# Two score groups on two partition halves: paired 64-row products in an attention kernel

## The chip, the cores and the metric

One core of a Trainium2 chip runs the whole program. The metric is the device time of one execution in microseconds, median of three runs.

## The reference, cut to what matters

A batch of 32 items with 128 tokens of 128 channels goes through a modulated linear layer, grouped-query attention (16 heads of width 64 in 4 groups that share keys and values), a second modulated layer with a small attention among the 16 heads of each token, a third modulated layer, and a top-2 mixture of 8 experts. The change is in the attention:

```python
Q = (X @ Wq).reshape(n, s, 4, 4, 64)      # group, head in group, key width
K = (X @ Wk).reshape(n, s, 4, 64)
V = (X @ Wv).reshape(n, s, 4, 64)
raw = einsum('bsgwe,btge->bstgw', Q, K / 8)
attn = softmax(raw, axis=2)               # over the keys t
A = einsum('bstgw,btge->bsgwe', attn, V).reshape(n, s, 1024)
return X + A @ Wpost
```

## The kernel before

The program is written engine by engine; each engine has its own queue in program order, and semaphores tie them. The batch is a software pipeline: slot s (function `slot` of each engine) does the attention core of item s (`B` in the code), projections of item s+1 (`A`), output projection and key mixing of item s-1 (`C`), head mixing of items s-2 and s-3 (`H`, `D`). Slots run from -2 to 34; those from 4 to 29 are a loop that does two slots a turn. Then come routing and an expert loop, in which this change touches nothing.

The scores are computed twice. First in bf16 with queries as rows (`scores`, L580): four products of 128x128 into the one bank `bank_s`, then VectorE takes the maximum over the keys (`group_max`, L292) into four columns of `row_max`. After four groups `row_max` is transposed by TensorE (L666), ScalarE negates it (`neg_max`), and GpSimd spreads it with a mask (L1053) into `neg_diag`: partition 64+h holds head h's negated maxima in its own quarter, zeros elsewhere. Then in fp32 with keys as rows (`scores_t`, L589): a bf16 product of `g_rows` with `neg_diag` starts the bank and puts minus the maximum everywhere, a fp32 product of keys and queries adds the scores. ScalarE takes the exponential out of the bank (`exp_scores`, into `prob`), and `attend` (L597) multiplies with the values; a column of ones gives the denominator, which VectorE inverts (L301) and applies (L306).

The contraction of keys and queries is 64 long, the array has 128 rows. Before, keys and queries of all groups lie on partitions 0 to 63, and partitions 64 to 127 of `qT`, `q16`, `k_one` and `k16` are zeros, so every product is one of 128 rows. Two groups leave the projection on partitions 0 to 63 and 64 to 127 of a bank; ScalarE's copies (`copy_q` L829 and the keys' copy) therefore come in two halves that bring the upper one down. The bf16 twins are made by ScalarE for the queries (`narrow_q`, L858) and by VectorE for the keys (L440). fp32 products appear in the trace as two records, each with its own weight load; bf16 products and transposes as one.

Three PSUM banks (`misc`) serve all the small results in turn; `bank_free` (L217) makes TensorE wait for the readers of a bank's last use. TensorE's order within a slot is written by hand (L644 to L742).

Of the kernel before, what the change touches and what calls it, by code (L numbers as in the profile page):

```python
# [19 lines left out]
HEADS = GROUPS * HPG  # L20
CHUNKS = HEADS * KEY // P
# [15 lines left out]
def build(nc, xT, condT, aff_wT, aff_b, mod_wT, mod_b, wq, wk, wv, wpost, gate_wT,  # L37
          w1, b1T, w2, b2, out):
    ctx = ExitStack()
    with ctx:  # L40
# [16 lines left out]
        own_head = sb("own_head", [P, HEADS])  # L57
        own_w = sb("own_w", [P, HPG])
# [30 lines left out]

        qT = sb("qT", [P, 2, HEADS, P])  # L90
        q16 = sb("q16", [P, 2, HEADS, P], BF16)
        k_one = sb("k_one", [P, 2, GROUPS, P])
        k16 = sb("k16", [P, 2, GROUPS, P], BF16)
# [81 lines left out]
        s_own, s_owned = sem("own"), sem("owned")  # L175
# [31 lines left out]
        def bank_users(bank, s):  # L207


            a, c, h, d = s + 1, s - 1, s - 2, s - 3  # L210
            return ((("q0", a, [(s_q, 4 * a + 2)]), ("q1", a, [(s_q, 4 * a + 4)]),
                     ("kv", a, [(s_v, n(a)), (s_k, 2 * n(a))]), ("y", a + 1, [(s_y_raw, n(a + 1))])),
                    (("att0", c, [(s_attT, 2 * c + 1)]), ("neg", s, [(s_neg, n(s))]), ("kx", c, [(s_kxT, n(c))]),
                     ("kxn", c, [(s_kx2, n(c))]), ("o", d, [(s_tok, n(d))])),
                    (("att1", c, [(s_attT, 2 * c + 2)]), ("post", c, [(s_x1T, n(c))]), ("mix", d, [(s_mixT, n(d))])))[bank]

        def bank_free(eng, bank, s, use):  # L217

            now = bank_users(bank, s)
            at = [u[0] for u in now].index(use)  # L220
            for _, b, readers in (*reversed(now[:at]), *reversed(bank_users(bank, s - 1))):
                if has(b):
                    for sm, v in readers:
                        eng.wait_ge(sm, v)
                    return

# [20 lines left out]
        def qkv_bank(b, use):  # L247

            return misc[("q0", "q1", "kv").index(use)] if s_is(b, 0) else misc[0]
# [5 lines left out]
        def _(dve):  # L255
# [3 lines left out]
            V.memset(k_one[KEY:P, :, :, :], 0.0).then_inc(s_zero, 1)  # L259
            V.memset(k16[KEY:P, :, :, :], 0.0).then_inc(s_zero, 1)  # L260
            V.memset(v1[:, :, :, :], 1.0).then_inc(s_zero, 1)
            V.memset(row_max[:, :], 0.0).then_inc(s_zero, 1)
            dve.wait_ge(s_const, 2)
            V.tensor_reduce(own_w[:, :], own_head[:, :].rearrange("p (g w) -> p w g", w=HPG), AX.X,
                            ALU.add).then_inc(s_owned, 1)
            V.tensor_reduce(own_g[:, :], own_head[:, :].rearrange("p (g w) -> p g w", w=HPG), AX.X,
# [22 lines left out]
            dve.wait_ge(s_zero, 6)  # L289
            dve.wait_ge(s_owned, 3)  # L290

            def group_max(s, g):  # L292
                dve.wait_ge(s_s_mm, 4 * s + g + 1)
                need(dve, s_neg_mm, n(s - 1))
                V.tensor_reduce(row_max[:, KEY + HPG * g:KEY + HPG * (g + 1)], bank_s[:, :, :], AX.X,  # L295
                                ALU.max).then_inc(s_max, 1)
# [56 lines left out]
            def slot(s, j):  # L353
# [3 lines left out]
                if B:  # L357
                    group_max(s, 3)
                if A:
                    dve.wait_ge(s_yT, n(a))  # L360
                    V.tensor_tensor(x_all[:, col(a)], x_all[:, col(a)], yT[:, :], ALU.add).then_inc(s_xy, 1)
                if D:
# [74 lines left out]
                if A:  # L437
                    dve.wait_ge(s_k, 2 * n(a))
                    need(dve, s_s_mm, 4 * n(a - 2))
# [3 lines left out]
                if B:  # L443
                    normalise(s, 0)
                if B:
                    invert(s, 1)
                if A:
                    group_max(a, 0)
                if B:
                    normalise(s, 1)  # L450
                if A:
                    group_max(a, 1)
                if B:
                    invert(s, 2)
                if B:
                    normalise(s, 2)
                if A:
                    group_max(a, 2)
                if B:
                    invert(s, 3)  # L460
                if B:
                    normalise(s, 3)
                if has(a + 1):
                    dve.wait_ge(s_y_raw, n(a + 1))
                    need(dve, s_kv_mm, n(a))
                    need(dve, s_xy, n(a))
                    V.tensor_scalar(yT[:, :], y_raw[:, :], CLAMP, -CLAMP, ALU.min, ALU.max).then_inc(s_yT, 1)  # L467

# [91 lines left out]
        def _(pe):  # L560
# [16 lines left out]
            pe.wait_ge(s_blank, 5)  # L577
# [28 lines left out]
            def queries(b, half):  # L606
                bank = qkv_bank(b, ("q0", "q1")[half])
# [17 lines left out]
            def gate_logits(tiles):  # L625

                bank = bank_s if tiles[0] in EARLY else misc[0]
                pe.wait_ge(s_tok, tiles[-1] + 1)
                for b in tiles:
# [14 lines left out]
            def slot(s, j):  # L644
# [5 lines left out]
                if C:  # L650
                    bank_free(pe, 1, s, "att0")
                    att_transpose(c, 0)
                if B:
                    scores(s, j, 3)
                if C:
                    bank_free(pe, 2, s, "att1")
# [3 lines left out]
                if A:  # L660
                    pe.wait_ge(s_yT, n(a))
                    queries(a, 0)
                if B:
                    bank_free(pe, 1, s, "neg")
                    pe.wait_ge(s_max, 4 * s + 4)
                    nc.tensor.transpose(misc[1][:, 0, :], row_max[:, :], ident[:, :]).then_inc(s_neg_mm, 1)  # L666
                if s_is(s, BATCH - 1):
                    gate_logits(parts_early[0])
                if C:
# [6 lines left out]
                    last.then_inc(s_post_mm, 1)  # L676
                if s_is(s, BATCH):
# [3 lines left out]
                if A:  # L681
                    if not s_is(a, 0):
                        bank_free(pe, 0, s, "q1")
                    queries(a, 1)
                if C:
                    bank_free(pe, 1, s, "kx")
# [4 lines left out]
                if B:  # L691
                    scores_t(s, j, 1)
                if C:
                    pe.wait_ge(s_kxT, n(c))
                    nc.tensor.transpose(misc[1][:, 0, :], kxT[:, :], ident[:, :]).then_inc(s_kxn_mm, 1)
                if D:
                    bank_free(pe, 2, s, "mix")
# [4 lines left out]
                if B:  # L702
                    attend(s, j, 0)
                if s_is(s, BATCH - 1):
# [407 lines left out]
```

## Time and profile before

| | |
|---|---|
| three runs | 666.54, 666.96, 669.44 us; median 666.96 |
| profiled execution | 666.56 us, of which the span 664.8 |
| TensorE, weight loads, VectorE, ScalarE, GpSimd busy | 92%, 73%, 78%, 62%, 43% of the span |
| TensorE's granted clock over the span | 0.972 of 2.4 GHz |
| bytes moved | 7.15 MB, nearly all in the first 25 us and the last 15 us |

The page's 40 slices show TensorE at nine tenths or more from the third slice to the 33rd (33 to 548 us), then a gap (the last items' mixing and the routing), and the expert loop after it. The loop of slots is thus where the time is. A record of TensorE has a modelled end that lies past the next record's start, so durations of records don't add up; distances between starts do. On VectorE and ScalarE too a record of a back-to-back row may reach some 0.1 us into the next one.

### The profile page before, as it was taken

Reading aid. Unit: us, or ns where it says so; the run is one execution under the profiler, and the core shown is the slowest. Engines: PE = TensorE matmul, PEld = TensorE weight load, DVE = VectorE, ACT = ScalarE, POOL = GpSimd, SP = SyncE. Lnnn points to the kernel's source line nnn. Section 1 sums busy time; section 2 is a strip of 40 time slices with the busy share of each in tenths; the row PEclk is TensorE's granted clock in tenths of the full one; section 3 lists DMA queues with packets and bytes.
Section 4 is the critical chain, followed back from the end, with each engine's and each line's share of the span. In section 5 each row is a group of like instructions: output and inputs, shape, how many; then the busy total and the mean of one; then the engine's idle time right before and its main releaser. Section 6 shows DMA issues by size and latency. Waiting matters only on the chain. (4 is left out here: it accounts for less than half of the span.)

```text
span 664.8 us, 14883 instructions
## 1 busy us (share of the span) xinstructions
PE 612.5 (92%) x4212; PEld 488.4 (73%) x4212; DVE 521.2 (78%) x1155; ACT 413.3 (62%) x823; POOL 287.8 (43%) x251
## 2 busy tenths in 40 slices
PE   3799999999999999999999999999999991699998
PEld 3587787777778777878787878787878780557665
DVE  6235888888888888888888888888888879867776
ACT  1666777777777767776666777777777541334443
POOL 5102555555555555555555555555555447000000
PEclk9799999999999999999999999999999995699999
DMA  7100000000000000000000000000000000000004
GB/s 246 45 1 1 1 2 1 1 0 0 0 0 0 0 0 0 0 0 0 0 0 0 0 0 0 0 0 0 0 0 0 2 1 0 1 0 0 0 0 126
DMA packets 9361, 7.15 MB, mean 11 GB/s; under 512 B 1088, under 2 KB 8832, under 8 KB 9216
## 3 DMA queue, kind: packets, MB, share of 16 engines
q1 hardware_dynamic: 9344, 6.94, 3.5%
q8 instruction: 9, 0.15, 0.1%
q14 instruction: 8, 0.07, 0.0%
HBM read 4.84 MB, written 2.10 MB: 10 GB/s over the span
## 5 line engine op out<-in xcount | busy, mean ns | idle before, releaser
L1061 POOL TENSOR_TENSOR pair<-kx 128x1152 f32<-128x1152 f32 x32 | 82.3, 2573 | 164.0 <-ACT kx L805 159.7
L602 PEld LDWEIGHTS bank_a<-v,prob 128*128 128x128 f32 x1024 | 127.1, 192 | 16.7 <-issue 16.2
L602 PE MATMUL bank_a<-v,prob 128*128 128x65 f32 x1024 | 131.7, 272 | 0.0
L594 PE MATMUL bank_t<-qT,k_one 128*128 128x512 f32 x256 | 131.6, 596 | 0.0
L295 DVE TENSOR_REDUCE row_max<-bank_s 128x4 f32<-128x512 f32 x128 | 87.3, 682 | 13.4 <-PE bank_s L585 9.0
L440 DVE CAST k<-k_one 64x512 bf16<-64x512 f32 x32 | 50.0, 1564 | 58.0 <-ACT k_one L805 58.0
L805 ACT ACTIVATE prob<-bank_t 128x512 f32<-128x512 f32 x128 | 76.3, 596 | 29.7 <-PE bank_t L594 26.5
L1041 POOL TENSOR_TENSOR mix_hi<-mix_hi 128x512 f32<-128x512 f32 (+2 forms) x96 | 80.0, 833 | 7.5
L609 PEld LDWEIGHTS misc<-yT,wq_sb 128*128 128x128 f32 x512 | 67.9, 200 | 18.3 <-issue 15.4
L1053 POOL TENSOR_TENSOR neg_diag<-neg_max,own_w 16x512 bf16<-16x512 f32 x32 | 36.3, 1134 | 100.8 <-ACT neg_max L805 86.4
L805 ACT ACTIVATE qT<-misc 64x512 f32<-64x512 f32 x128 | 75.4, 589 | 5.9 <-PE misc L609 3.5
L609 PE MATMUL misc<-yT,wq_sb 128*128 128x128 f32 x512 | 71.1, 285 | 2.4 <-DVE yT L467 2.4
L805 ACT ACTIVATE q<-qT 64x1024 bf16<-64x1024 f32 x64 | 67.2, 1050 | 1.0
L1034 POOL TENSOR_TENSOR mix_hi<-weight,kx 128x1024 f32<-128x1024 f32 x32 | 63.9, 1998 | 4.7 <-ACT weight L805 4.7
L585 PEld LDWEIGHTS bank_s<-k,q 128*128 128x128 bf16 x512 | 33.9, 98 | 40.8 <-DVE row_max L295 20.6
L585 PE MATMUL bank_s<-k,q 128*128 128x128 bf16 x512 | 50.5, 221 | 14.2 <-DVE k L440 12.3
L674 PE MATMUL misc<-attT,wpost_sb 128*128 128x128 f32 x512 | 62.6, 275 | 0.0
L306 DVE TENSOR_TENSOR att<-bank_a,recip_den 128x256 f32<-128x256 f32 x128 | 54.1, 423 | 9.9
L674 PEld LDWEIGHTS misc<-attT,wpost_sb 128*128 128x128 f32 x512 | 60.3, 193 | 0.0
L805 ACT ACTIVATE y_raw<-misc,modb_sb,demod 128x128 f32<-128x128 f32 x32 | 14.6, 457 | 68.8 <-PE misc L739 66.8
L805 ACT ACTIVATE hT<-bank_t,b_now 128x512 f32<-128x512 f32 x42 | 28.9, 687 | 44.7 <-PE bank_t L771 44.6
L594 PEld LDWEIGHTS bank_t<-qT,k_one 128*128 128x128 f32 x256 | 49.1, 192 | 4.6
(153 smaller groups left out, 1069.9 us busy)
## 6 DMA issues: line engine op xcount, KB each, us to landing
out<-acc_all SPq DMA_DIRECT2D x8, 256.0 KB, 2.3
x_all<-in_xT SPq DMA_DIRECT2D x1, 1024.0 KB, 9.8
w_sb<-in_w SPq DMA_DIRECT2D x2, 512.0 KB
x_all<-in_xT SPq DMA_DIRECT2D x1, 768.0 KB, 7.6
wq_sb<-in_wq SPq DMA_DIRECT2D x1, 512.0 KB, 6.2
wpost_sb<-in_wpost SPq DMA_DIRECT2D x1, 512.0 KB, 9.5
x_all<-in_xT SPq DMA_DIRECT2D x1, 256.0 KB, 3.3
b_rows<-in_b SPq DMA_DIRECT2D x16, 4.0 KB
```

The source lines that it names most:

```text
L295: V.tensor_reduce(row_max[:, KEY + HPG * g:KEY + HPG * (g + 1)], bank_s[:, :, :], AX.X, ALU.max).then_inc(s_max, 1)
L306: V.tensor_tensor(att[:, HPG * g:HPG * (g + 1), :], att_bank(g)[:, :, 0:KEY], recip_den[:, g % 2, :].unsqueeze(2).to_broadcast([P, HPG, KEY]),
L440: V.tensor_copy(k16[0:KEY, ja, :, :], k_one[0:KEY, ja, :, :]).then_inc(s_k16, 1)
L585: last = mm(bank_s[:, w, :], q16[:, j, HPG * g + w, :], k16[:, j, g, :], start=(w == 0), stop=True, skip_group_check=True)
L594: mm(bank_t[g % 2][:, :, :], k_one[:, j, g, :], qT[:, j, HPG * g:HPG * (g + 1), :], start=False, stop=True).then_inc(s_t_mm, 1)
L602: last = mm(att_bank(g)[:, w, :], prob[:, g % 2, w, :], v1[:, j, g, :], start=(w == 0), stop=True, skip_group_check=True)
L609: last = mm(bank[:, c % 4, :], wq_sb[:, c * P:(c + 1) * P], yT[:, :], start=(c % 4 == 0), stop=True, skip_group_check=True)
L674: last = mm(misc[2][:, 0, :], wpost_sb[:, k, :], attT[:, k, :], start=(k == 0), stop=(k == CHUNKS - 1))
L805: return nc.scalar.activation(out_, in_, func, **kw)
L1034: G.tensor_tensor(mix_hi[:, :, :].rearrange("p r (h e) -> p r h e", e=MD), weight[:, jd, MH // 2:MH, :].unsqueeze(3).to_broadcast([P, MH / ...
L1041: G.tensor_tensor(mix_hi[:, 0:r, :], mix_hi[:, 0:r, :], mix_hi[:, r:2 * r, :], ALU.add).then_inc(s_hi, 1)
L1061: G.tensor_tensor(pair[:, :, :], bass.AP(kx2, jc * 2 * P, [[4 * P, P], [0, SHIFTS], [1, P]]), bass.AP(kx2, jc * 2 * P, [[4 * P, P], [MD, S ...
```

## The change

Groups 2p and 2p+1 stay where the projection leaves them, on partitions 0 to 63 and 64 to 127 (`wq` is permuted on the host so that head w of both groups lies in one block). No zeros pad them; copies and narrowing span 128 partitions; the keys' narrowing goes to ScalarE. Each score product is one of 64 rows. `scores_t` does a pair of groups at once: a bf16 product on each half, one into each of the two banks, then fp32 products of two heads (256 columns), alternating between the halves. `group_max` writes bf16 maxima on a diagonal of a tile of four planes that is zero elsewhere; four bf16 products with the identity transpose them into `bank_s`, where they are already spread, and one ScalarE copy negates them into `neg_diag`; GpSimd has no part in it. TensorE's order in a slot is new, VectorE's and ScalarE's follow; `bank_free` gives way to waits written out.

```diff
-        row_max = sb("row_max", [P, P])
-        neg_max = sb("neg_max", [P, P])
+        row_max = sb("row_max", [P, HPG, P], BF16)
...
+                V.tensor_reduce(bass.AP(row_max, max_row(g), [[HPG * P, P], [P + 1, HPG]]).unsqueeze(2),
+                                bank_s[:, :, :], AX.X, ALU.max).then_inc(s_max, 1)
...
             def scores(s, j, g):
                 need(pe, s_max, 4 * s + g)
+                if g == 0:
+                    need(pe, s_neg, s)
                 pe.wait_ge(s_q16, 2 * s + g // 2 + 1)
+                rows = slice(KEY * (g % 2), KEY * (g % 2 + 1))
                 for w in range(HPG):
-                    last = mm(bank_s[:, w, :], q16[:, j, HPG * g + w, :], k16[:, j, g, :],
+                    last = mm(bank_s[:, w, :], q16[rows, j, g // 2, w, :], k16[rows, j, g // 2, :],
                               start=(w == 0), stop=True, skip_group_check=True)
...
-            def scores_t(s, j, g):
-                need(pe, s_prob, 4 * s + g - 1)
-                pe.wait_ge(s_own, n(s))
-                mm(bank_t[g % 2][:, :, :], g_rows[:, g, :], neg_diag[:, j, :, :], start=True, stop=False)
-                mm(bank_t[g % 2][:, :, :], k_one[:, j, g, :], qT[:, j, HPG * g:HPG * (g + 1), :],
-                   start=False, stop=True).then_inc(s_t_mm, 1)
+            def scores_t(s, j, p):
+                need(pe, s_prob, 4 * s + 2 * p)
+                pe.wait_ge(s_neg, n(s))
+                for half in range(2):
+                    rows = slice(KEY * half, KEY * (half + 1))
+                    mm(bank_t[half][:, :, :], g_rows[rows, 2 * p + half, :], neg_diag[rows, j, :, :],
+                       start=True, stop=True, skip_group_check=True)
+                for w in range(0, HPG, 2):
+                    for half in range(2):
+                        rows = slice(KEY * half, KEY * (half + 1))
+                        last = mm(bank_t[half][:, w:w + 2, :], kT[rows, j, p, :], qT[rows, j, p, w:w + 2, :],
+                                  start=False, stop=True, skip_group_check=True)
+                        if w == HPG - 2:
+                            last.then_inc(s_t_mm, 1)
...
-                    nc.tensor.transpose(misc[1][:, 0, :], row_max[:, :], ident[:, :]).then_inc(s_neg_mm, 1)
+                    for w in range(HPG):
+                        last = mm(bank_s[:, w, :], row_max[:, w, :], ident16[:, :],
+                                  start=(w == 0), stop=True, skip_group_check=True)
+                    last.then_inc(s_neg_mm, 1)
...
-                for par in range(2):
-                    f(qT[0:KEY, j, HEADS // 2 * half + par:HEADS // 2 * (half + 1):2, :],
-                      qkv_bank(b, ("q0", "q1")[half])[par * KEY:(par + 1) * KEY, :, :]).then_inc(s_q, 1)
+                f(qT[:, j, half, :, :], misc[half][:, :, :]).then_inc(s_q, 1)
...
-                    f(neg_max[KEY:KEY + HEADS, :], misc[1][KEY:KEY + HEADS, 0, :], scale=-1.0).then_inc(s_neg, 1)
+                    f(neg_diag[:, j, :, :], bank_s[:, :, :], scale=-1.0).then_inc(s_neg, 1)
...
-                    V.tensor_copy(k16[0:KEY, ja, :, :], k_one[0:KEY, ja, :, :]).then_inc(s_k16, 1)
+                    f(k16[:, ja, :, :], misc[0][:, 0:2, :]).then_inc(s_k16, 1)
...
-                    G.tensor_tensor(neg_diag[rows, j, :, :],
-                                    neg_max[rows, :].unsqueeze(1).to_broadcast([HEADS, HPG, P]),
-                                    own_w[rows, :].unsqueeze(2).to_broadcast([HEADS, HPG, P]),
-                                    ALU.mult).then_inc(s_own, 1)
...
-            G.memset(q16[KEY:P, :, :, :], 0.0).then_inc(s_blank, 1)
-            G.memset(qT[KEY:P, :, :, :], 0.0).then_inc(s_blank, 1)
-            G.memset(neg_diag[:, :, :, :], 0.0).then_inc(s_blank, 1)
```

The order of TensorE's steps in a slot, by the functions' names (numbers are groups or halves, `pair` is the new `scores_t`; the y product is the one of item s+2):

```
before: att_T 0, scores 3, att_T 1, queries 0, row max, post, scores_t 0, queries 1, kx, scores_t 1,
        kxn, mix_T, attend 0, keys/values, o, scores_t 2, attend 1, scores 0, scores_t 3, scores 1,
        attend 2, scores 2, attend 3, y
after:  att_T 0, queries 0, scores 3, att_T 1, queries 1, row max, post, pair 0, keys/values, kx,
        attend 0, attend 1, kxn, y, mix_T, pair 1, scores 0, o, attend 2, scores 1, attend 3, scores 2
```

In the new order VectorE clips y into `yT` (L467) between `normalise` 1 and `group_max` 0 of the next item, where before it was the slot's last step; ScalarE copies the keys, `kxT`, `k16`, values, `kx2`, `y_raw`, `mixT` and `weight` between the second and the third exponential.

## Rows read from the trace of the kernel before

**Rows 1.** the page's busy line: engine, busy us, share of the span, instructions

```profile
PE 612.5 (92%) x4212; PEld 488.4 (73%) x4212; DVE 521.2 (78%) x1155; ACT 413.3 (62%) x823; POOL 287.8 (43%) x251
```

**Rows 2.** stretch table, one slot of the loop; the page's busy columns, granted clock, DMA

```profile
300.00:316.00 16.00, 15.66 (x117) 12.82 (x116) 13.57 (x30) 11.42 (x23) 8.48 (x7) 1.00 0.00 0
```

**Rows 3.** TensorE's timeline of one slot: start us, us, engine, line, operation, count

```profile
300.26 0.44 PE L739 MATMUL misc<-xs,modw_sb 128*128 128x128 f32 x2
...
301.32 0.63 PE L616 MATMUL misc<-ident,att 128*128 128x128 f32 x4
301.79 1.06 PE L609 MATMUL misc<-yT,wq_sb 128*128 128x128 f32 x8
302.69 0.27 PE L666 MATMUL misc<-ident,row_max 128*128 128x128 f32 x1
302.79 1.95 PE L674 MATMUL misc<-attT,wpost_sb 128*128 128x128 f32 x16
304.60 0.38 PE L593 MATMUL bank_t<-neg_diag,g_rows 128*128 128x512 bf16 x1
304.82 1.02 PE L594 MATMUL bank_t<-qT,k_one 128*128 128x512 f32 x2
305.67 1.05 PE L609 MATMUL misc<-yT,wq_sb 128*128 128x128 f32 x8
...
308.08 1.00 PE L602 MATMUL bank_a<-v,prob 128*128 128x65 f32 x8
308.92 0.66 PE L711 MATMUL misc<-yT,wk_sb 128*128 128x128 f32 x4
...
309.93 0.46 PE L718 MATMUL misc<-mixT,modw_sb 128*128 128x128 f32 x2
...
311.30 1.00 PE L602 MATMUL bank_a<-v,prob 128*128 128x65 f32 x8
312.64 0.39 PE L585 MATMUL bank_s<-k,q 128*128 128x128 bf16 x4 [0.34 <-DVE k L440]
312.87 0.38 PE L593 MATMUL bank_t<-neg_diag,g_rows 128*128 128x512 bf16 x1
...
316.31 0.44 PE L739 MATMUL misc<-xs,modw_sb 128*128 128x128 f32 x2
```

**Rows 4.** groups by form, the 64-row products of before

```profile
L566 PE MATMUL misc<-cond_sb,affw_sb 64*128 64x32 f32 x6 | 1.5, 401 | 4.5 <-DMA modb_sb<-in_mod_b 4.5
```

**Rows 5.** groups by form, whole span: busy us, mean ns of one

```profile
L805 ACT ACTIVATE qT<-misc 64x512 f32<-64x512 f32 x128 | 75.4, 589 | 5.9 <-PE misc L609 3.5
...
L805 ACT ACTIVATE q<-qT 64x1024 bf16<-64x1024 f32 x64 | 67.2, 1050 | 1.0
...
L805 ACT ACTIVATE k_one<-misc 64x256 f32<-64x256 f32 x64 | 24.2, 379 | 10.8 <-PE misc L713 10.0
```

**Rows 6.** GpSimd's timeline of the same slot

```profile
303.42 1.03 POOL L1053 TENSOR_TENSOR neg_diag<-neg_max,own_w 16x512 bf16<-16x512 f32 x1 [2.10 <-ACT neg_max L805]
309.66 2.57 POOL L1061 TENSOR_TENSOR pair<-kx 128x1152 f32<-128x1152 f32 x1 [5.20 <-ACT kx L805]
```

**Rows 7.** VectorE's timeline of the same slot

```profile
302.30 1.22 DVE L365 TENSOR_TENSOR mix_lo<-weight,kx 128x1024 f32<-128x1024 f32 x1
...
309.21 0.43 DVE L421 TENSOR_TENSOR shifted<-score,h_max 128x256 f32<-128x256 f32 x1
310.87 1.64 DVE L440 CAST k<-k_one 64x512 bf16<-64x512 f32 x1 [1.22 <-ACT k_one L805]
...
313.13 0.66 DVE L295 TENSOR_REDUCE row_max<-bank_s 128x4 f32<-128x512 f32 x1
```

**Rows 8.** timeline of the start, all engines

```profile
5.80 3.16 DVE L269 CAST g_rows<-own_g 128x512 bf16<-128x512 f32 x1
...
13.77 0.46 ACT L805 ACTIVATE y_raw<-misc,modb_sb,demod 128x128 f32<-128x128 f32 x1 [2.03 <-DVE demod L288]
...
21.13 0.42 DVE L440 CAST k<-k_one 64x512 bf16<-64x512 f32 x1 [6.21 <-ACT k_one L805]
```

More of the change, by code:

```diff
@@ L205, in has @@
             return not isinstance(b, int) or 0 <= b < BATCH
[L207 to L225, printed above, removed]
         def slots(eng, slot):
@@ L467, in slot @@
                     V.tensor_scalar(yT[:, :], y_raw[:, :], CLAMP, -CLAMP, ALU.min, ALU.max).then_inc(s_yT, 1)
+                if A:
+                    group_max(a, 0)
+                if B:
+                    invert(s, 2)
+                    normalise(s, 2)
+                if A:
+                    group_max(a, 1)
+                if B:
+                    invert(s, 3)
+                    normalise(s, 3)
+                if A:
+                    group_max(a, 2)
             slots(dve, slot)
@@ L606, in queries @@
             def queries(b, half):
-                bank = qkv_bank(b, ("q0", "q1")[half])
+                bank = misc[half]
                 for c in range(4 * half, 4 * half + 4):
@@ L650, in slot @@
                 if C:
-                    bank_free(pe, 1, s, "att0")
+                    if s_is(c, 0):
+                        pe.wait_ge(s_q, 2 * n(s))
+                    need(pe, s_kx2, c)
                     att_transpose(c, 0)
+                if A:
+                    pe.wait_ge(s_yT, n(a))
+                    if has(d - 1):
+                        pe.wait_ge(s_tok, d)
+                    queries(a, 0)
                 if B:
@@ L681, in slot @@
                 if A:
-                    if not s_is(a, 0):
-                        bank_free(pe, 0, s, "q1")
-                    queries(a, 1)
+                    pe.wait_ge(s_q, 2 * a + 1)
+                    bank = misc[0]
+                    for i in range(2):
+                        mm(bank[:, i, :], wk_sb[:, i * P:(i + 1) * P], yT[:, :],
+                           start=(i == 0), stop=True, skip_group_check=True)
+                    mm(bank[:, 2:4, :].rearrange("p a f -> p (a f)"), yT[:, :], wv_sb[:, :], start=False,
+                       stop=True, skip_group_check=True).then_inc(s_kv_mm, 1)
                 if C:
-                    bank_free(pe, 1, s, "kx")
+                    if A:
+                        pe.wait_ge(s_q, 2 * a + 2)
                     pe.wait_ge(s_x1s, n(c))
@@ L702, in slot @@
                 if B:
[L703 to L722 removed]
+                    scores_t(s, j, 1)
                 if A:
@@ L725, in slot @@
                     scores(a, ja, 0)
+                if D:
+                    pe.wait_ge(s_mixT, n(d))
+                    if has(a + 1):
+                        pe.wait_ge(s_y_raw, n(a + 1))
+                    need(pe, s_tok, d)
+                    mm(misc[0][:, 0, :], modw_sb[:, 2, :], mixT[:, :], start=True, stop=True).then_inc(s_o_mm, 1)
                 if B:
-                    scores_t(s, j, 3)
+                    attend(s, j, 2)
                 if A:
@@ L949, in slot @@
                       bias=modb_sb[:, 0:1]).then_inc(s_y_raw, 1)
+                if D:
+                    act.wait_ge(s_mixT_mm, n(d))
+                    need(act, s_o_mm, n(d - 1))
+                    act.wait_ge(s_style, 3)
+                    f(mixT[:, :], misc[2][:, 0, :], scale=style[:, 2, bass.ds(d, 1)]).then_inc(s_mixT, 1)
+                if s_is(s, BATCH):
+                    copy_logits(EARLY, 6)
+                if not late(s):
+                    head_weights()
+                if B:
+                    exp_scores(s, 2)
+                    exp_scores(s, 3)
+                if D:
+                    act.wait_ge(s_o_mm, n(d))
+                    act.wait_ge(s_demod, 5)
+                    f(tok_all[:, col(d)], misc[0][:, 0, :], ACT.Identity, scale=demod[:, 2, bass.ds(d, 1)],
+                      bias=modb_sb[:, 2:3]).then_inc(s_tok, 1)
                 if s_is(s, BATCH + 2):
```

202 lines of the change are left out of this document (69 added, 133 removed).

## The prediction

> **What bounds the kernel now.** I read the page's busy line first: TensorE is busy 92% of the span, VectorE 78%, ScalarE 62%, GpSimd 43% [rows 1]. Then the stretch table of one slot in the loop: 15.66 of 16 us busy on TensorE at a granted clock of 1.00 (2.4 GHz) [rows 2]; VectorE has 13.57, ScalarE 11.42, GpSimd 8.48. Then the TensorE timeline of a whole slot, which is the view to trust: a record's own length overlaps the next, so I cost each group by the distance from its first start to the next group's first start [rows 3]. The first product of y comes at 300.26 and again at 316.31, so a slot takes 16.05 us, and 30 slots (1 to 30) have that shape: 481 us of the 664.8. The profiled execution took 666.56 us (span plus 1.8), 0.4 under the median 666.96 of the three runs; the sum is made against 666.6 and holds for the median as well.
>
> From those distances one slot asks of TensorE: a four-record transpose group 0.47, eight records of a query group 0.89, the row-maximum transpose 0.10, sixteen records of the output projection 1.81, the bf16 row-maximum product 0.22, the two fp32 records of 512 columns 0.85, eight records of attend 0.84, keys and values together 1.01, four bf16 score records 0.23 [rows 3]. Two-record products are 0.23 (eight records take 0.84 to 0.89). Summed: transposes 0.9, queries 1.78, scores 0.92, row maximum 0.10, projection 1.81, transposed scores 4 x 1.07 = 4.28, attend 3.36, keys and values 1.01, the three modulated products 0.69, the two single transposes 0.22: 15.1 us. So about 0.95 us of a slot is waiting; the largest part is the attend group that takes 1.34 where another takes 0.84: the scores behind it wait for the bf16 keys [rows 3]. TensorE sets the slot, and a small chain through VectorE adds to it.
>
> **The change, part by part.** *Paired transposed scores.* Before, each group is one bf16 product (0.22) and one fp32 product over 128 rows whose lower 64 are zeros, as two records of 0.43 each: 1.07. After, a pair of groups is two bf16 products on rows 0 to 63 and 64 to 127, then four fp32 products of 256 columns that alternate between the halves, so eight records of 0.215. If neighbours on different halves run together, each record is paired with its neighbour except the first and the last (the two records of one product share a half): 5 steps of 0.215, plus 0.22 for the bf16 pair, is 1.30 a pair, 2.60 a slot, against 4.28. If they don't, it is 10 x 0.215 = 2.15 a pair, 4.30 a slot. No row of before has two products on different halves: its only 64-row products are the six small ones at the start [rows 4], on one half, each behind the other. So the price lies between -1.68 and +0.02 us a slot. I take the whole gain as the likelier, since neighbours that alternate share neither partitions nor PSUM bank, but nothing in the trace proves it.
>
> The Trainium skill (TensorEngine Tiling (Array Packing), Key Properties) says that row tiles on different rows run independently, loads and products both; the trace of before can't show it. The same section says that changing the tiling mode drains TensorE. It speaks against this change, and the second rival prices it from rows.
>
> *Switches between 128-row and 64-row products.* The new order has five stretches of 64-row work a slot (scores 3; pair 0; pair 1 with scores 0; scores 1; scores 2): ten switches, two of them (into scores 1 and 2) behind a wait anyway, eight exposed. Bounds for one: nothing, or the tail of a record that back-to-back work hides, 0.285 long against a distance of 0.11, so 0.17 [rows 3], plus a weight load that isn't prefetched, 0.1, the distance of two records: 0.27. I take nothing, the nearest rows being the changes from fp32 to bf16 groups inside a slot, which cost nothing that shows.
>
> *Row maxima.* One fp32 transpose (0.10) becomes four bf16 products into bank_s (0.23): +0.13 on TensorE. Behind it ScalarE's negation grows from 16x128 to 128x512, priced by the qT copy of 512 elements, 0.59 [rows 5], some 0.3 more, and GpSimd's neg_diag (1.03, [rows 6]) goes. The chain to the transposed scores is shorter by 0.7, but the projection's 1.81 covers it in both.
>
> *Copies.* Query copies go from four of 0.59 to two of the same length over 128 partitions, the narrowing from two of 1.05 to two of 0.6 [rows 5], the key copies from 2 x 0.38 to one [rows 5], the narrowing of keys comes over from VectorE at 0.38. ScalarE: -1.2 -0.9 -0.4 +0.4 +0.3 = -1.8 us a slot, off the bound. VectorE loses its key cast of 1.64 [rows 7], and with it the wait on TensorE.
>
> *The new order.* With TensorE at 15.1 - 1.68 + 0.13 = 13.55, what is late next must be walked. Latencies from rows: from the end of a TensorE group to its reader 0.27 (scores from 312.64 to 312.87, row_max starts 313.13), from a reader's end to the next product 0.13 [rows 3, 7]. Let 0 be the start of pair 0. Pair 0 ends 1.30, keys and values 2.31, the x1 product 2.54, attend 0 and 1 4.22 (their exponentials, 0.6 each like the qT copy, end 1.96 and 2.56), kxn 4.33, y 4.56, mix transpose 4.67, pair 1 5.97, scores 0 6.20, o 6.43. ScalarE runs exp 0 and 1, key copy, kxT, k16, v (4.2), kx2 (5.0), y_raw (5.4), mixT (5.8), weight (6.2), then exp 2 ends 6.8: attend 2 runs 6.94 to 7.78, 0.5 late. VectorE: from mix_lo's start to the end of shifted is 7.3 us in a slot [rows 7], so it is done about 4.9, and invert and normalise 0 and 1 by 6.3. Then comes yT, now ahead of the first row maximum. GpSimd's pair product of 2.57 [rows 6] starts when kx2 is out, 5.1, and ends 7.7. In before VectorE's key cast, 0.42 long alone [rows 8], started inside that product and took 1.64, ending 0.28 behind it [rows 6, 7]. yT is a copy-like step between SBUF tiles too, so I let it end at 7.9; row maximum 0 then ends 8.6, scores 1 starts 8.73 (0.95 late), attend 3 ends 9.80, row maximum 1 9.98, scores 2 starts 10.11 (0.3 late), then transposes, query group 0, scores 3 (11.67), transposes, query group 1 (13.23), row maxima 13.46, projection 15.27. The period is about 15.2: 13.55 of work and 1.7 of waiting, against 16.05. The Trainium skill (SBUF — State Buffer, "SBUF: two separate sides") calls this an exclusive lock of a shared port pair, held for the whole instruction; by it a VectorE step in a two-port mode waits for GpSimd, and the cast's row agrees.
> Without that collision the same walk gives 14.75.
>
> *Start and end.* The GpSimd memsets of q16, qT and neg_diag go. The cast of g_rows, 3.16 us beside them [rows 8], should fall to about 0.5, so the demodulation chain to the first y_raw at 13.77 [rows 8] could start 2.7 earlier; TensorE also waits for the query weights before its first product, whose landing no row here bounds from below, so between 0 and -2.7, and I take -1.5. Slot 0, partly at 1.2 GHz, and slot 31 gain about 1.4 each from their pairs. Slots past 32, routing and the expert loop are not touched: 0.
>
> **Sum.** 30 x 0.85 = 25.5, plus 1.5 + 2.8 = 4.3: 29.8. 666.6 - 29.8 = 636.8 us; with 14.75, 623. I forecast 637.
>
> **Rivals.** (1) *The halves don't run together.* Pair 0 then costs 0.85 more in full; pair 1's 0.85 is mostly absorbed, since scores 1 is waiting for the row maximum anyway. Period 15.2 + 0.85 = 16.05, as before; the start gains 2 to 3: about 664, between 655 and 673. For it: no row shows concurrency. Against: neighbours share neither rows nor bank. (2) *Switching costs, the slower side.* If each of the eight exposed switches costs the hidden tail, 0.17, that is 1.36 a slot: period 16.56, 666.6 + 30 x 0.51 - 4.3 = 678; with the unprefetched load, 0.27, it is 2.16 a slot, period 17.4, 702. It turns the sign from 0.85 / 8 = 0.11 us a switch upward. For it: the records' tails really are 0.17 long and hidden only because work of one shape follows; against: only that bf16 and fp32 groups change without cost. The drain rule of the Trainium skill's tiling page would bring this about; the page gives no length. (3) *Pairs work, but another VectorE step falls into the GpSimd product.* Shifted ends at 4.9 and the product starts at 5.1; if VectorE is 0.3 late there, that step takes up to 2.5 more and delays weight, exp 2 and all behind, some 0.5 us more a slot after what waits there already: period 15.7, 652. (4) *The change doesn't do what it says*: the one part that may be there in name only is the pairing, and that is rival 1; the removed casts and memsets vanish from the program whatever the chip does.
>
> **Chances.** Forecast case (with and without the yT collision, small switch costs), 618 to 650: 0.53. Rival 3, 650 to 663: 0.09. Rival 1, 655 to 673: 0.16, of which 0.03 faster, 0.09 the same, 0.04 slower. Rival 2, 668 to 702: 0.22. Within 0.5% (3.3 us, about what a measurement of this kernel can tell from no change) there is 0.09; faster 0.53 + 0.09 + 0.03 = 0.65; slower 0.22 + 0.04 = 0.26. For 8 in 10 the range takes the forecast case from 618 and reaches through the lower half of rival 2, to 682.
>
> **What would show each step right or wrong.** In the timeline of a slot after: the distance from the first record of a pair to the next group, 1.3 if halves run together, 2.15 if not. The distance from scores into the group behind and from the group before into scores: 0.23 and unchanged if switches are free, 0.1 to 0.3 more each if not. yT's duration: 0.23 or over 1. The wait of scores 1 and 2 for row_max: about 0.95 and 0.3 us. ScalarE busy about 1.8 less a slot, GpSimd 1.0 less, the slot period 15.2. First y_raw near 12.2. The prediction is wrong if the period is set by something that no step above names, or if TensorE's clock leaves 1.00 in the loop since it idles more.

## The result and the profile after

The changed kernel takes 888.42 us against 666.75: a ratio of 1.333, 95% interval 1.330 to 1.336. I had forecast 637 with a range of 618 to 682. It is slower by 222 us where 30 faster was expected, and no rival of mine reached it either.

The page of the changed kernel: the busy line, TensorE's share and its granted clock over 40 slices.

```profile
PE 744.2 (84%) x4564; PEld 619.4 (70%) x4564; DVE 465.0 (52%) x1121; ACT 354.5 (40%) x759; POOL 239.1 (27%) x216
...
PE   4988888888889988888888888899888889559998
...
PEclk9866777777777666667777777776666679858999
```

ScalarE is down from 413 to 354.5 us and GpSimd from 288 to 239, as the parts of the sum said. But VectorE is at 52% of the span where it was 78% [rows 1], so nothing there is the new bound, and TensorE's clock is 0.6 to 0.7 through nearly the whole loop where it was 1.00 [rows 2]. Two things are wrong at once: TensorE waits, and it is slow.

TensorE's timeline of one slot of the changed kernel, against [rows 3] (start us, us, engine, line, operation; in brackets the idle time before it and what ended it); at the end two GpSimd rows and a ScalarE row of the same slot.

```profile
306.79 0.39 PE L566 MATMUL bank_t<-neg_diag,g_rows 64*128 64x512 bf16 x2
307.02 1.03 PE L571 MATMUL bank_t<-qT,kT 64*128 64x256 f32 x8
307.97 0.71 PE L679 MATMUL misc<-yT,wk_sb 128*128 128x128 f32 x4
...
310.91 0.28 PE L698 MATMUL misc<-ident,kxT 128*128 128x128 f32 x1
...
314.87 0.80 PE L704 MATMUL misc<-xs,modw_sb 128*128 128x128 f32 x2 [3.69 <-POOL xs L1008]
...
315.82 0.61 PE L566 MATMUL bank_t<-neg_diag,g_rows 64*128 64x512 bf16 x2
316.22 1.92 PE L571 MATMUL bank_t<-qT,kT 64*128 64x256 f32 x8
317.92 0.63 PE L556 MATMUL bank_s<-k,q 64*128 64x128 bf16 x4
...
330.76 0.39 PE L566 MATMUL bank_t<-neg_diag,g_rows 64*128 64x512 bf16 x2
```

```profile
311.37 0.38 ACT L797 ACTIVATE kx<-misc 128x256 f32<-128x256 f32 x1 [0.89 <-PE misc L698]
...
311.91 2.56 POOL L1026 TENSOR_TENSOR pair<-kx 128x1152 f32<-128x1152 f32 x1 [14.33 <-ACT kx L797]
...
314.42 0.40 POOL L1008 TENSOR_TENSOR xs<-x_all,style 128x128 f32 x1
```

The y product (L704) stands idle 3.69 us for `xs`. GpSimd makes xs behind its pair product, and the pair product waits for this slot's kx2 (L797 `kx`), which comes from the transpose at 310.91. So TensorE issues that transpose, the result goes through ScalarE, then 2.56 us of GpSimd, then 0.40, and only then may TensorE go on. Before, the y product was the last step of a slot, far behind. Pair 0 at full clock takes 1.18 us up to the next group, pair 1 behind the wait 2.1: TensorE takes about twice as long there. The stretch table of the same slot (columns: stretch, its length, busy us and counts of TensorE, weight loads, VectorE, ScalarE, GpSimd, granted clock, DMA share, GB/s):

```profile
303.00:307.00 4.00, 4.00 (x35) 3.84 (x36) 2.92 (x4) 3.15 (x6) 0.00 (x0) 0.93 0.00 0
307.00:311.00 4.00, 4.00 (x35) 3.54 (x31) 3.71 (x10) 2.72 (x7) 0.00 (x0) 1.00 0.00 0
311.00:314.80 3.80, 0.19 (x2) 0.00 (x0) 1.75 (x6) 0.38 (x1) 2.89 (x2) 0.86 0.00 0
314.80:318.00 3.20, 3.13 (x14) 2.17 (x15) 0.23 (x1) 1.03 (x3) 1.11 (x2) 0.50 0.00 0
318.00:324.00 6.00, 6.00 (x33) 5.17 (x31) 2.46 (x7) 1.54 (x3) 3.31 (x4) 0.50 0.00 0
324.00:327.00 3.00, 3.00 (x16) 2.64 (x15) 0.86 (x3) 0.82 (x2) 0.00 (x0) 0.50 0.00 0
```

The clock falls to 0.50 (1.2 GHz) near the end of the idle stretch and comes back 13.65 us later; the next idle stretch begins 8 us after that. This slot takes 24.0 us (pair 0 to pair 0), the mean over 100 to 500 us is 23.9.

### The profile page after: what moved, and what is told of

It is laid out like the page before. It is cut to its first block and busy times, and to the rows that moved or that the text cites. A ratio compares the mean times of both kernels' runs of the same rounds, so it can differ in the third digit from the quotient of the medians.

```text
span 888.2 us, 15301 instructions
## 1 busy us (share of the span) xinstructions
PE 744.2 (84%) x4564; PEld 619.4 (70%) x4564; DVE 465.0 (52%) x1121; ACT 354.5 (40%) x759; POOL 239.1 (27%) x216
## 5 line engine op out<-in xcount | busy, mean ns | idle before, releaser
L581 PE MATMUL bank_a<-v,prob 128*128 128x65 f32 x1024 | 177.3, 337 | 2.3 <-ACT prob L797 2.2
L581 PEld LDWEIGHTS bank_a<-v,prob 128*128 128x128 f32 x1024 | 170.0, 254 | 9.9 <-issue 5.7
L272 DVE TENSOR_REDUCE row_max<-bank_s 128x4 bf16<-128x512 f32 x128 | 88.8, 694 | 132.0 <-PE bank_s L556 132.0
L704 PE MATMUL misc<-xs,modw_sb 128*128 128x128 f32 x64 | 24.7, 488 | 107.8 <-POOL xs L1008 103.6
L797 ACT ACTIVATE attT<-misc 128x512 f32<-128x512 f32 x64 | 38.2, 597 | 174.7 <-PE misc L595 174.7
L588 PE MATMUL misc<-yT,wq_sb 128*128 128x128 f32 x512 | 96.0, 349 | 1.1 <-DVE yT L423 1.1
L704 PEld LDWEIGHTS misc<-xs,modw_sb 128*128 128x128 f32 x64 | 15.7, 304 | 113.8 <-POOL xs L1008 97.8
L571 PE MATMUL bank_t<-qT,kT 64*128 64x256 f32 x512 | 91.5, 492 | 0.0
L797 ACT ACTIVATE prob<-bank_t 128x512 f32<-128x512 f32 x128 | 69.5, 594 | 51.1 <-PE bank_t L571 51.1
L556 PE MATMUL bank_s<-k,q 64*128 64x128 bf16 x512 | 76.1, 300 | 2.3 <-DVE row_max L272 2.3
L571 PEld LDWEIGHTS bank_t<-qT,kT 64*128 64x128 f32 x512 | 65.5, 251 | 10.3
L556 PEld LDWEIGHTS bank_s<-k,q 64*128 64x128 bf16 x512 | 47.4, 129 | 28.2 <-issue 14.8
L797 ACT ACTIVATE y_raw<-misc,modb_sb,demod 128x128 f32<-128x128 f32 x32 | 14.6, 457 | 121.1 <-PE misc L704 121.1
L595 PE MATMUL misc<-ident,att 128*128 128x128 f32 x256 | 61.5, 383 | 0.5 <-DVE att L283 0.5
```

Of the source, the lines that this page charges most:

```text
L272: V.tensor_reduce(bass.AP(row_max, max_row(g), [[HPG * P, P], [P + 1, HPG]]).unsqueeze(2), bank_s[:, :, :], AX.X, ALU.max).then_inc(s_max, 1)
L556: last = mm(bank_s[:, w, :], q16[rows, j, g // 2, w, :], k16[rows, j, g // 2, :], start=(w == 0), stop=True, skip_group_check=True)
L571: last = mm(bank_t[half][:, w:w + 2, :], kT[rows, j, p, :], qT[rows, j, p, w:w + 2, :], start=False, stop=True, skip_group_check=True)
L581: last = mm(att_bank(g)[:, w, :], prob[:, g % 2, w, :], v1[:, j, g, :], start=(w == 0), stop=True, skip_group_check=True)
L588: last = mm(bank[:, c % 4, :], wq_sb[:, c * P:(c + 1) * P], yT[:, :], start=(c % 4 == 0), stop=True, skip_group_check=True)
L595: last = nc.tensor.transpose(misc[1 + half][:, c % 4, :], att[:, 2 * c:2 * c + 2, :].rearrange("p h e -> p (h e)"), ident[:, :])
```

## The experiments

Two theories stood against each other. Q: the place of y against GpSimd's queue makes the wait, and the idle time makes the low clock. A: the array itself, that is 64-row products and the switching between shapes, costs time or lowers the clock.

**xs moved ahead of the pair product** in GpSimd's queue (e_xs_first).

```diff
+                if has(s + 2):
+                    xs_of(s + 2, j)
                 if C:
                     pool.wait_ge(s_kx2, n(c))
...
-                if has(s + 2):
-                    xs_of(s + 2, j)
```

> The changed kernel with one step of GpSimd's queue moved: the scaling of x for item s+2 (xs) now stands ahead of the pair product of item s-1, not behind it. Nothing else changes. Theory Q (queue order and clock): TensorE's y product, moved up in the new order, waits 3.7 us a slot for xs, which stands behind the 2.6 us pair product, which itself waits for this slot's kx; and the idle time lets the clock fall to 1.2 GHz for 13.65 of each 23.9 us, which costs another 6.8. Without that wait the slot should take 14.6 to 15.2 us and the kernel 615 to 635 us, with a granted clock near 0.97. Theory A (the array): half-filled 64-row products or the switching between 64 and 128 rows keep the clock low or cost time of their own; then only the wait goes, and the kernel takes about 888 - 30 x 3.7 = 777 us with the clock still near 0.75.

Measured 686.25 us, ratio to before 1.030 (1.026 to 1.034). The wait for xs is gone, and 202 of the 222 us with it. But 686 is between what the two theories gave, and the clock is still not 1.00: over 100 to 500 us it is 0.90, against 0.71 in the changed kernel. A slot from TensorE's timeline with the step that stands out, then two VectorE rows of the same slot:

```profile
313.33 0.39 PE L566 MATMUL bank_t<-neg_diag,g_rows 64*128 64x512 bf16 x2
...
321.55 0.40 PE L556 MATMUL bank_s<-k,q 64*128 64x128 bf16 x4 [0.52 <-DVE row_max L272]
...
328.68 0.39 PE L566 MATMUL bank_t<-neg_diag,g_rows 64*128 64x512 bf16 x2
```

```profile
319.44 1.45 DVE L423 TENSOR_SCALAR yT<-y_raw 128x128 f32<-128x128 f32 x1
320.81 0.68 DVE L272 TENSOR_REDUCE row_max<-bank_s 128x4 bf16<-128x512 f32 x1
```

This slot lies at full clock and takes 15.35 us, 0.08 from the walk in the prediction; yT starts inside GpSimd's pair product (318.23 to 320.81) and takes 1.45, so scores 1 waits. Most slots have a low stretch of 3.4 us, some in the middle of the loop share one of 6.8; the mean slot over 100 to 500 us is 16.9 us.

**The same wait put into the kernel before** (e_before_wait): one wait, no 64-row product in the slots.

```diff
                     nc.tensor.transpose(misc[1][:, 0, :], kxT[:, :], ident[:, :]).then_inc(s_kxn_mm, 1)
+                if has(a + 1):
+                    pe.wait_ge(s_xs, n(a + 1))
```

> The kernel before with one wait added and nothing else: behind the transpose of kxT TensorE waits until xs of item s+2 is written, as the changed order makes it wait. No 64-row product, no pairing. Theory Q: TensorE reaches the wait at 308.0 in the old trace and xs comes at about 312.5, so 4.5 us of idle time a slot, less the 0.5 to 0.9 that the slot waited anyway; if idle time is what lowers the clock, a low stretch of 13.65 us a slot costs 6.8 more: slot about 26.5, kernel 960 to 990 us, clock about 0.75. Theory A: without 64-row products the clock stays at 1.00 in the loop and only the wait is added: 666 + 30 x 3.7 = about 780 us.

Measured 864.26 us, ratio 1.296 (1.291 to 1.301): one wait alone gives nine tenths of the change's loss. TensorE idles 4.5 us a slot (the row below), and the clock falls in a kernel whose score products are all of 128 rows:

```profile
304.78 0.47 PE L701 MATMUL misc<-ident,mix 128*128 128x128 f32 x1 [4.56 <-POOL xs L1030]
```

```profile
300.00:304.70 4.70, 0.22 (x2) 0.00 (x0) 1.68 (x5) 1.56 (x4) 2.91 (x2) 0.89 0.00 0
304.70:309.00 4.30, 4.22 (x18) 3.97 (x19) 0.00 (x0) 0.58 (x2) 0.00 (x0) 0.50 0.00 0
309.00:312.00 3.00, 3.00 (x17) 2.15 (x16) 1.10 (x4) 2.95 (x7) 1.10 (x1) 0.76 0.00 0
312.00:316.00 4.00, 4.00 (x34) 3.30 (x33) 3.27 (x9) 0.80 (x3) 3.31 (x4) 1.00 0.00 0
```

The expected number (960 to 990) was too high: the low stretch is 3.4 or 6.8 us here, not 13.65, and the clock over the loop 0.87. Idle time lowers the clock, but it alone doesn't set how long the clock stays low.

**The wait filled with work** (e_filler): the changed kernel with 16 fp32 products ahead of the wait, into `bank_s`, which is free then.

```diff
+                if has(a + 1) and C:
+                    for i in range(16):
+                        mm(bank_s[:, i % HPG, :], modw_sb[:, 0, :], ident[:, :],
+                           start=(i % HPG == 0), stop=True, skip_group_check=True)
                 if has(a + 1):
...
                     pe.wait_ge(s_xs, n(a + 1))
```

> The changed kernel, with 16 products of 128x128 in fp32 (32 records, 3.5 us at 2.4 GHz) of constant tiles put into bank_s ahead of the wait for xs; their result is overwritten and never read, so the work is extra and the output is the same. It keeps the wait's length and takes away only the idleness of TensorE. Theory Q: the clock stays at 1.00, the slot takes 23.9 - 6.8 = 17.1 us, kernel about 684 us although it does more work. Theory A: the clock is low for another reason, about 888 us as the changed kernel, or more.

Measured 739.93 us, ratio to before 1.109; the clock is 1.00 through the loop. 3.6 us a slot more work (the 32 records stand from 312.56 to 316.20, and y follows without a wait) makes the changed kernel 148.5 us shorter. That is the price of the low clock by itself: 148.5 / 30 = 4.95 us a slot. My 684 charged the clock half of the whole low stretch, 6.8, too much since part of the stretch is idle anyway.

**Halves not alternating** (e_halves_apart): e_xs_first with both fp32 products of one half first, then both of the other.

```diff
-                for w in range(0, HPG, 2):
-                    for half in range(2):
+                for half in range(2):
+                    for w in range(0, HPG, 2):
```

> The kernel e_xs_first with the fp32 products of a pair reordered: both products of the lower half first, then both of the upper half, instead of alternating. Same work, same number of records. If products on different halves run together as the changed kernel's trace suggests (a pair takes 1.18 us where ten records one after the other would take 2.15), only one step of seven to eight now overlaps: a pair takes about 1.75, up to 1.1 us a slot more, of which some falls into waits: 15 to 30 us over e_xs_first. If the short pair has another reason (records that cost less with 64 rows), both kernels take the same time within 0.5%.

Measured 688.59 us against 686.25, the intervals overlap. A pair 1 of this kernel, then of e_xs_first:

```profile
301.50 0.39 PE L566 MATMUL bank_t<-neg_diag,g_rows 64*128 64x512 bf16 x2
301.73 1.13 PE L571 MATMUL bank_t<-qT,kT 64*128 64x256 f32 x8
302.59 0.38 PE L556 MATMUL bank_s<-k,q 64*128 64x128 bf16 x4
```

```profile
300.90 0.39 PE L566 MATMUL bank_t<-neg_diag,g_rows 64*128 64x512 bf16 x2
301.12 1.03 PE L571 MATMUL bank_t<-qT,kT 64*128 64x256 f32 x8
301.99 0.38 PE L556 MATMUL bank_s<-k,q 64*128 64x128 bf16 x4
```

Eight fp32 records take 0.86 and 0.87 us: the order makes no difference, as my second reading said (688.59 is within 0.5% of 686.25). But a third reading, which I hadn't written down, gives that too. Either a 64-row record is cheap by itself, or the two halves run as two streams of four records, 4 x 0.215 = 0.86, whatever the order of issue. The next runs decide between them.

**64-row products alone** in the kernel before: first the bf16 scores (e_before_64s), then the fp32 scores as well (e_before_64st), all on the lower half, nothing that could pair.

```diff
-                    last = mm(bank_s[:, w, :], q16[:, j, HPG * g + w, :], k16[:, j, g, :],
+                    last = mm(bank_s[:, w, :], q16[0:KEY, j, HPG * g + w, :], k16[0:KEY, j, g, :],
...
-                mm(bank_t[g % 2][:, :, :], k_one[:, j, g, :], qT[:, j, HPG * g:HPG * (g + 1), :],
+                mm(bank_t[g % 2][:, :, :], k_one[0:KEY, j, g, :], qT[0:KEY, j, HPG * g:HPG * (g + 1), :],
```

> The kernel before with only the bf16 score products cut to the 64 partitions that hold data (scores use rows 0 to 63 of q16 and k16; the zeros are no longer read). Same order, same count, all on one half: it adds eight switches between 128-row and 64-row work a slot and nothing else. In the changed kernel's trace a group of four takes 0.31 to 0.32 us to the next group where before it took 0.23, and the group ahead of it about 0.1 more. If a switch costs 0.1 us: 0.4 to 0.8 us a slot, kernel 678 to 690 us, clock unchanged at 1.00 in the loop. If switches are free: within 0.5% of before. If 64-row products alone lower the clock: low stretches appear in the loop and the kernel takes over 700 us.

> e_before_64s with the fp32 score product cut to rows 0 to 63 as well, still one product of 512 columns a group, all on the same half, so nothing can run in pairs. It tells why a pair is short in the changed kernel (eight fp32 records of 256 columns take 0.87 us whether their halves alternate or not). Theory P (two halves run together): a lone 64-row record of 512 columns takes 0.43 us as before, the group 1.07 plus switches: kernel 4 to 20 us over e_before_64s. Theory R (an fp32 record of 64 rows streams at twice the rate of one of 128 rows): the two records take 0.43 us together instead of 0.85, up to 1.7 us a slot less, some of it given back by eight more switches: kernel 30 to 50 us under e_before_64s, 635 to 660 us.

Measured 684.05 us (ratio 1.027, 1.024 to 1.030) and 709.65 (1.066, 1.063 to 1.068). Less data is read and the kernel is slower, by 17.5 and another 25.6 us. The clock is 1.00 in the loop in both, so 64-row products don't lower it. The first adds eight switches in each of some 31 slots: 17.5 / 248 = 0.07 us each in the kernel's time. The second adds six, not eight, because scores 1, which stands behind the last of its fp32 products, has 64 rows too: 25.6 / 186 = 0.14 us each. Theory P had 4 to 20 us for this step; it is more, but on P's side, and R's 30 to 50 us less is out. In the timelines the groups around a switch come about 0.1 us later each. Two groups of e_before_64s, then the score product of e_before_64st:

```profile
307.74 0.39 PE L585 MATMUL bank_s<-k,q 64*128 64x128 bf16 x4
308.07 1.11 PE L602 MATMUL bank_a<-v,prob 128*128 128x65 f32 x8
309.01 0.44 PE L739 MATMUL misc<-xs,modw_sb 128*128 128x128 f32 x2
```

```profile
300.37 0.39 PE L593 MATMUL bank_t<-neg_diag,g_rows 128*128 128x512 bf16 x1
300.69 1.12 PE L594 MATMUL bank_t<-qT,k_one 64*128 64x512 f32 x2
301.65 0.38 PE L585 MATMUL bank_s<-k,q 64*128 64x128 bf16 x4
```

A score group takes 0.33 to the next where it took 0.23 [rows 3]. The bf16 product ahead of the lone fp32 product takes 0.32 where it took 0.22, and the fp32 product itself 0.96 with 64-row scores behind it (1.05 ahead of a 128-row group), not half of 0.85. So a 64-row record isn't cheap by itself, and the pair's 0.86 for twice the work is two halves running at once. Together with the order test this says two streams. The single records agree: in e_xs_first they start two by two, 4 ns apart and 0.215 us from one two to the next.

**Row maximum 0 ahead of yT** (e_max_first): e_xs_first with one swap on VectorE.

```diff
+                if A:
+                    group_max(a, 0)
                 if has(a + 1):
                     dve.wait_ge(s_y_raw, n(a + 1))
...
-                if A:
-                    group_max(a, 0)
```

> e_xs_first with one swap in VectorE's order: the row maximum of group 0 now stands ahead of the clip into yT instead of behind it. In e_xs_first yT takes 1.45 us (0.23 when alone) because it starts inside GpSimd's pair product, and scores 1 waits 0.5 to 0.8 us for the row maximum behind it. Theory L (the shared port and the idle time it makes): the maximum reads PSUM and isn't held, so scores 1 starts about 0.6 earlier, the slot at full clock falls from 15.35 to about 14.8, and with the idle time gone the low-clock stretch (3.4 us in each 17.07) goes too: kernel 630 to 640 us, clock 0.97. Theory S (64-row products or thin work keep the clock falling): the low stretch stays, slot about 16.4, kernel 665 to 670 us.

Measured 628.92 us, ratio 0.942 (0.940 to 0.945): it beats both kernels, by a little more than theory L gave. Pair 0 to pair 0 takes 14.82 us, the wait of scores 1 is all but gone (0.4 us, once between 172 and 492), and the clock over 100 to 500 us is 0.99:

```profile
300.14 0.39 PE L566 MATMUL bank_t<-neg_diag,g_rows 64*128 64x512 bf16 x2
...
314.96 0.39 PE L566 MATMUL bank_t<-neg_diag,g_rows 64*128 64x512 bf16 x2
```

```profile
305.35 2.58 POOL L1032 TENSOR_TENSOR pair<-kx 128x1152 f32<-128x1152 f32 x1 [7.81 <-ACT kx L797]
...
306.31 0.70 DVE L272 TENSOR_REDUCE row_max<-bank_s 128x4 bf16<-128x512 f32 x1
306.92 1.08 DVE L425 TENSOR_SCALAR yT<-y_raw 128x128 f32<-128x128 f32 x1
```

```profile
100.00:500.00 400.00, 394.18 (x3338) 341.71 (x3339) 345.54 (x745) 249.04 (x551) 203.46 (x156) 0.99 0.00 0
```

The row maximum keeps its 0.70 inside the pair product. yT is still held (1.08), but now nothing on TensorE waits for it in time.

**The small wait filled** (e_fill_max): e_xs_first with eight fp32 records ahead of scores 1, into `misc[1]`; the VectorE order isn't touched.

```diff
+                if A and C and B:
+                    pe.wait_ge(s_kx2, n(c))
+                    for i in range(4):
+                        mm(misc[1][:, i, :], modw_sb[:, 0, :], ident[:, :],
+                           start=(i == 0), stop=True, skip_group_check=True)
                 if A:
                     scores(a, ja, 1)
```

> e_xs_first with 4 fp32 products of 128x128 (8 records, 0.85 us) put ahead of scores 1 into a bank that is free then; never read, output unchanged. They fill the wait for the row maximum. Theory L: the clock stays at 1.00 in the loop and the slot takes 15.4 to 15.8 us, kernel 645 to 655 us: faster than e_xs_first although it works more. Theory S: the clock falls as before and the extra work comes on top: 686 to 700 us.

Measured 650.73 us (0.977, 0.975 to 0.980), clock 1.00 in the loop. More work, 35 us shorter than e_xs_first: the low stretch of that kernel came from a wait of 0.5 to 0.8 us, between 65-column attend records and 64-row scores.

**y moved instead of xs** (e_y_mid): GpSimd's queue as in the changed kernel; on TensorE y stands between scores 1 and attend 3, on VectorE yT behind row maximum 1, on ScalarE y_raw last.

```diff
                 if A:
                     scores(a, ja, 1)
+                if has(a + 1):
+                    if D:
+                        pe.wait_ge(s_tok, n(d))
+                    elif A:
+                        pe.wait_ge(s_v, n(a))
+                        pe.wait_ge(s_k16, n(a))
+                    pe.wait_ge(s_xs, n(a + 1))
+                    mm(misc[0][:, 0, :], modw_sb[:, 0, :], xs[:, j, :], start=True, stop=True).then_inc(s_y_mm, 1)
                 if B:
                     attend(s, j, 3)
```

> The changed kernel with GpSimd's queue left as it is and the y product moved down instead: on TensorE it stands between scores 1 and attend 3 (about 8.9 us into the slot, when GpSimd's pair product and xs are over), on ScalarE y_raw stands last, on VectorE the clip into yT stands behind row maximum 1, so row maximum 0 isn't held up. Theory Q: the loss comes from where y stands against GpSimd's queue, whichever side is moved; the wait for xs is gone, the clock stays at 1.00 and the slot takes 14.7 to 15.2 us: 625 to 642 us, near the 629 of e_max_first. If xs behind the pair product is late in itself, or the chain y, y_raw, yT, queries 0 is now too short, the slot takes over 15.5 us and the clock falls again: over 655 us.

Measured 632.81 us (0.951, 0.947 to 0.955), clock 1.00; the wait for xs is at most 0.3 us. The same cure from the other side: neither step is at fault alone, their order against each other is.

**Dense work behind the wait** (e_dense): the changed kernel with four fp32 products of 512 columns right behind y.

```diff
+                if A and C:
+                    for i in range(4):
+                        mm(bank_s[:, :, :], modw_sb[:, 0, :], wq_sb[:, 0:512], start=True, stop=True)
```

> The changed kernel with four fp32 products of 512 columns of constant tiles (8 records, 3.4 us at 2.4 GHz) put right behind the y product, so behind the 3.7 us wait; never read, output unchanged. It asks why the clock stays low for 13.65 us of each slot there, when the kernel before with the same wait has it low for only 3.4 or 6.8. Theory D: what TensorE does behind the wait decides; in the kernel before it is long fp32 records, in the changed kernel 64-row products, short attend records and small gaps. Then with dense work behind the wait the low stretch shrinks to 3.4 or 6.8 us, the granted clock in the loop rises from 0.71 to 0.85 or more, and the kernel takes 870 to 920 us although it has 3.4 us more work a slot. Theory E: the wait alone decides; the low stretch stays at 13.65 or grows, clock 0.70, kernel 990 to 1040 us.

Measured 902.66 us in one round (1.353, 1.344 to 1.363). The wait is as long as in the changed kernel (3.68 us before y). The clock over 100 to 500 us rises to 0.92:

```profile
100.00:500.00 400.00, 336.15 (x2224) 247.57 (x2223) 197.74 (x466) 159.74 (x349) 124.39 (x102) 0.92 0.00 0
```

3.4 us a slot of extra work cost 14 us instead of 102, since most low stretches shrink to 3.4 us. So what follows the idle time decides how long the clock stays low: it is back after 3.4 us behind long fp32 records, and after 13.65 behind the changed kernel's own mixture of 64-row products, short attend records and gaps.

## Why the prediction was wrong

**The step that failed.** In "The new order" I let the y product run from 4.33 to 4.56, without asking for its input xs. In the same paragraph I let GpSimd's pair product run from 5.1 to 7.7, and xs stands behind it in GpSimd's queue; [rows 6] has the product that must end first. With xs at 0.40 my own walk would have started y at 8.2, a wait of 3.9 us; the trace has 3.69. I had walked TensorE, ScalarE and VectorE, and of GpSimd only what collides with VectorE, not what it delivers.

**The clock.** I kept 1.00 and named its fall only as a thing that would make me wrong, with no price. It is the larger part of the loss. From 628.9 us (e_max_first), the wait with its time filled adds 111 us (739.9, e_filler), and the same wait idle another 148.5 (888.4). The swap on VectorE isn't in the last two, but yT isn't held there either (0.23 in both), so the 111 is nearly all the wait: 30 x 3.7.

This term fails the sum even without the wait for xs. e_xs_first is in effect the kernel that my walk described, with its period (15.35 against 15.2), and it takes 686, not 637: the wait of scores 1, which the walk had as 0.95 us of harmless waiting, brings the clock down too. The sign of the forecast comes true only where that wait is removed or filled as well (629, 633 and 651 us).

**Terms of the sum**, each against what the runs show:
- Pairs: 1.30 expected, 1.09 to 1.18 measured. The mechanism was right, its form was not: the halves run as two streams, not as neighbours in steps, and alternating gains nothing. Rival 1 is excluded.
- Switches: nothing expected, 0.07 us each in the time of e_before_64s and about 0.10 in the timelines, so 0.7 to 1.0 a slot for ten. Rival 2's mechanism is real at about half its price. By itself it is as large as the 0.85 a slot that I forecast as the gain; the shorter pairs and the shorter wait of scores 1 pay for it. The Trainium skill (TensorEngine Tiling (Array Packing), Key Properties) has both rules, independent tiles and a drain at a change of mode, and these runs agree with both.
- The period at full clock: 15.2 expected, 15.35 in e_xs_first, and 14.75 without the yT collision, 14.82 in e_max_first. The closeness is in part luck, errors that cancel: switches +0.8, pairs -0.3, and the wait of scores 1 was 0.5 to 0.8, not 0.95.
- The collision of yT: "0.23 or over 1". In the changed kernel it is 0.23, because the wait for xs has moved it behind the pair product; with the wait gone it is 1.45 (median 1.50 of 32). What was read off the key cast [rows 7] held for yT.
- ScalarE -1.8 a slot: (413.3 - 354.5) / 32 = 1.84. GpSimd: 287.8 - 239.1 = 48.7 us, the 36.3 of neg_diag and the memsets most of it. First y_raw "near 12.2": 12.31.
- The slot that I read in the kernel before, 16.05, is a short one; the mean over 100 to 500 us is 16.20, and 15.05 in e_max_first.

**Open.** Why the clock in e_max_first still falls twice in the loop was not looked into. Which of the thin records (64 rows, attend's 65 columns, or the gaps between) keep it low after an idle stretch was not separated. The kernel before waits 0.34 us a slot at a clock of 1.00, and so does e_before_64s (0.33), ahead of 64-row scores; e_xs_first waits 0.5 to 0.8 and has low stretches. Whether the length of the wait alone makes the difference, no run tells.

## What to carry to other kernels

When a step moves in one engine's order, write down for each of its inputs the queue that makes it and what stands ahead of it there; if the thing ahead waits for this slot's own results, the move closes a loop through other engines. Price idle time on TensorE twice, once as time and once as clock: here 3.7 us of idle time a slot cost 8.65 ((888.4 - 628.9) / 30). And don't treat half a microsecond of waiting in the middle of short records as small: filling it with unused products gained 35 us, and the swap of two lines on VectorE that removed it gained 57.

## What the runs showed of the hardware

- Idle time of 3.7 to 4.5 us a slot took TensorE from 2.4 to 1.2 GHz in kernels with and without 64-row products; in e_xs_first a wait of 0.5 to 0.8 us behind short records did too, in most slots for 3.4 us. Work behind the wait set the way back: 13.65 us low in the changed kernel, 3.4 to 6.8 in the kernel before with the same wait, mostly 3.4 with dense fp32 records behind it.
- 64-row fp32 products on different halves and banks run at once, eight records of 256 columns in 0.86 us, alternating or not. A lone 64-row product is no faster than one of 128 rows: 0.96 us against 0.85 to the next group (e_before_64st).
- A change between 128-row and 64-row products costs about 0.10 us in the timelines; in the kernel's time it was 0.07 (e_before_64s) and 0.14 (the six of e_before_64st). Padding the contraction with zeros, as the kernel before does, is the cheaper form of an unpaired product.
- A 128x128 fp32 clip between SBUF tiles on VectorE took 1.45 us instead of 0.23 beside a GpSimd product; the row maximum, which reads PSUM, kept its 0.70 there (e_max_first).
